# Single rows of the node table fetched by SyncE and ScalarE for 14 gather tiles in place of 5, in a graph attention layer

## The reference

```python
Q, K, V = (x @ Wq + bq), (x @ Wk + bk), (x @ Wv + bv)        # [N, 8 heads, 12]
E = edge_attr @ We + be                                      # [edges, 8, 12]
score = K[src] * Q[dst] / sqrt(12) * E
score = exp(clip(score.sum(-1), -5, 5))                      # [edges, 8]
msg = V[src] * score
h = segment_sum(msg, dst) / (segment_sum(score, dst) + 1e-6)
out = layernorm(x + h)
```

## Time and profile before

| | |
|---|---|
| median of the runs | 999.71 us |
| the profiled execution, its own time | 999.58 us |
| its span, first to last instruction | 997.9 us |
| GpSimd (POOL) busy | 741.4 us, 74% |
| VectorE (DVE) busy | 651.9 us, 65% |
| TensorE (PE) busy | 646.7 us, 65% |
| ScalarE (ACT) busy | 186.5 us, 19% |
| DMA | 165.62 MB, mean 166 GB/s |

### The profile page before, as it was taken

The page is one execution under the profiler, slowest core; times in us unless marked ns, Lnnn a source line. Parts: engine busy times, 40 slices in busy tenths (PEclk is TensorE's granted clock), DMA queues, the critical chain, the costliest instruction groups (busy, mean ns, idle before and its releaser), DMA issues. The chain is left out here.

```text
span 997.9 us, 13968 instructions
## 1 busy us (share of the span) xinstructions
PE 646.7 (65%) x3276; PEld 418.5 (42%) x3276; DVE 651.9 (65%) x1307; ACT 186.5 (19%) x373; POOL 741.4 (74%) x783
## 2 busy tenths in 40 slices
PE   5688778656655665748566666567657664757663
PEld 5564555433433443435333343344434443434443
DVE  6637999666756665766565766566756666657665
ACT  4742222111111111111111111111111111111111
POOL 7777777777777777777777777777777777777772
PEclk9888999888877887886878787877887788887885
DMA  6899776665656556555656556565565565665531
GB/s 196 286 293 244 197 203 176 177 184 156 176 143 170 155 146 177 156 153 159 168 145 167 148 147 171 152 162 156 157 176 142 145 174 149 162 160 140 143 86 42
DMA packets 102425, 165.62 MB, mean 166 GB/s; under 512 B 45725, under 2 KB 65006, under 8 KB 102335
## 3 DMA queue, kind: packets, MB, share of 16 engines
q1 hardware_dynamic: 64399, 84.88, 30.8%
q0 software_dynamic: 36784, 74.86, 28.6%
q10 hardware_dynamic: 1152, 4.92, 1.4%
HBM read 152.18 MB, written 12.39 MB: 165 GB/s over the span
## 5 line engine op out<-in xcount | busy, mean ns | idle before, releaser
L419 POOL DMA_INDIRECT kv<-kv_table,idx x745 | 709.8, 953 | 227.1 <-issue 225.9
L522 PE MATMUL psT<-identity,qe 96*128 96x96 f32 x782 | 111.8, 301 | 292.0 <-DVE qe L861 291.9
L944 DVE TENSOR_TENSOR qke<-psT,kv 128x768 f32<-128x768 f32 (+1 forms) x99 | 93.6, 945 | 288.6 <-DMA kv<-kv_table,idx 287.1
L501 PE MATMUL psE<-ea,we 97*96 97x512 f32 x392 | 268.8, 825 | 0.8 <-ACT kv L641 0.8
L522 PEld LDWEIGHTS psT<-identity,qe 96*128 96x128 f32 x782 | 89.2, 172 | 308.6 <-DVE qe L861 308.4
L571 PEld LDWEIGHTS psA<-place,msg 128*104 128x104 f32 x1536 | 159.9, 179 | 36.0 <-DVE msg L971 26.0
L571 PE MATMUL psA<-place,msg 128*104 128x104 f32 x1536 | 167.0, 264 | 9.9 <-DVE msg L971 9.5
L671 ACT ACTIVATE qe<-psE 96x1024 f32<-96x1024 f32 (+1 forms) x99 | 99.8, 1009 | 231.2 <-PE psE L501 231.2
L685 ACT ACTIVATE msg<-clipped 128x64 f32<-128x64 f32 (+1 forms) x99 | 25.3, 255 | 513.4 <-DVE clipped L959 503.4
L861 DVE TENSOR_TENSOR qe<-psQ,qe 96x1024 f32<-96x1024 f32 (+1 forms) x99 | 118.5, 1197 | 3.7 <-ACT qe L671 3.6
L501 PEld LDWEIGHTS psE<-ea,we 97*96 97x96 f32 x392 | 77.8, 224 | 82.8 <-issue 82.8
(11 more groups left out here) (105 smaller groups left out, 324.9 us busy)
## 6 DMA issues: line engine op xcount, KB each, us to landing
ea<-eaT SPq DMA_DIRECT2D x99, 384.0 KB, 4.1
q_parts<-rel_table SPq DMA_DIRECT2D x99, 252.0 KB
kv<-kv_table,idx POOLq DMA_INDIRECT x745
kv_rows<-kv_table SPq DMA_DIRECT2D x640, 0.8 KB
qwin<-q_table SPq DMA_DIRECT2D x198, 23.6 KB
xb<-xrows SPq DMA_DIRECT2D x24, 144.0 KB
out<-ob SPq DMA_DIRECT2D x24, 144.0 KB
kv_table<-kv ACTq DMA_DIRECT2D x2, 960.0 KB, 8.3
```

Of the source, the lines that this page charges most:

```text
L419: pool.indirect_dma_start(kv[:, k, t], None, kv_table, sources).then_inc(kv_in[k], 16)
L501: last = nc.tensor.matmul(psE[0:D, h, 0:size], we[:], ea[:, k % EAR, edge:edge + size], start=True, stop=True)
L522: last = nc.tensor.transpose(psT[:, t % 2, t // 2 * D:(t // 2 + 1) * D], qe[0:D, k % 2, t * P:(t + 1) * P], identity[0:D, 0:D])
L944: nc.vector.tensor_tensor(qke[:, 0:nt].rearrange("p (t b) d -> p b t d", **by_bank), psT[:, :, 0:nt // 2 * D].rearrange("p b (t d) -> p b ...
```

## The change

14 tiles in place of 5 are left out by GpSimd. Nine of them, those of groups 15, 25, ..., 95, are SyncE's: 13 rows in a turn, 10 turns for a tile (the last has 11 rows), in groups 4 to 93 without a gap. Five, those of groups 22, 38, ..., 86, are ScalarE's: 8 rows in a turn, 16 turns for a tile, in groups 4 to 83, issued by ScalarE after its moves and before the two functions of the root. Both begin in group 4. The buffer `kv_rows` is no tensor of its own any more but lies in `q_full`, which nothing reads after the first stage; ScalarE's first turn waits for that (`q_up`). The list of source numbers that is loaded once, `row_id`, grows from 640 to 1792 numbers. VectorE waits for `rows_up` in 14 groups.

```diff
-BY_ROW = (24, 40, 56, 72, 88)
-ROWS = 8
+SP_ROWS, ACT_ROWS = 13, 8
+SP_TURNS, ACT_TURNS = -(-P // SP_ROWS), -(-P // ACT_ROWS)
+FROM = 4
+SP_TILES = tuple(15 + SP_TURNS * i for i in range(9))
+ACT_TILES = tuple(22 + ACT_TURNS * i for i in range(5))
+BY_ROW = SP_TILES + ACT_TILES
...
-        kv_rows = sb("kv_rows", [P, len(BY_ROW), 2 * D], f32)
+        kv_rows = q_full[:].rearrange("p t d -> p (t d)").rearrange("p (i f) -> p i f", f=2 * D)[:, 0:len(BY_ROW)]
...
+        def load_single_rows(eng, i, j, rows):
+
+            count = min(rows, P - j * rows)
+            edge = i * P + j * rows
+            nodes = nc.values_load_multi_w_load_instructions(
+                row_id[0:1, edge:edge + count], engines=[eng.engine], min_val=0, max_val=N - 1,
+                skip_runtime_bounds_check_because="source nodes of edges are nodes")[1]
+            for p in range(count):
+                eng.dma_start(kv_rows[j * rows + p:j * rows + p + 1, i], kv_table[bass.ds(nodes[p], 1), :]
+                              ).then_inc(rows_in[i], 16)
...
-                        turn = at - (BY_ROW[0] - P // ROWS - 1)
-                        if 0 <= turn < len(BY_ROW) * P // ROWS:
-                            load_single_rows(turn)
+                        turn = at - FROM
+                        if turn == 0:
+                            sp.wait_ge(row_id_in, 16)
+                            sp.wait_ge(kv_out, 16 * len(KV_CHUNKS))
+                        if 0 <= turn < len(SP_TILES) * SP_TURNS:
+                            load_single_rows(sp, turn // SP_TURNS, turn % SP_TURNS, SP_ROWS)
...
+                        turn = at - FROM
+                        if first and turn == 0:
+                            act.wait_ge(row_id_in, 16)
+                            act.wait_ge(q_up, NR // P // QB)
+                        if first and 0 <= turn < len(ACT_TILES) * ACT_TURNS:
+                            load_single_rows(act, len(SP_TILES) + turn // ACT_TURNS, turn % ACT_TURNS, ACT_ROWS)
                         if first and BG <= at < NG and at % BG == 1:
                             block_rstd(U // BG * r + k // BG - 1, BC)
...
-                                dve.wait_ge(rows_up, BY_ROW.index(at) + 1)
+                                dve.wait_ge(rows_up, sum(1 for x in BY_ROW if x <= at))
```

More of the change, by code:

```diff
@@ L333, in _ @@
                     ahead = []
[L335 to L346, removed]
                     def loads(r, k, at):
```

## The result

The changed kernel takes **1137.35 us** (median of 4 runs, 1136.43 to 1139.88) against 999.7 us before (4 runs, 999.14 to 1000.49). The ratio is 1.138, with a 95% interval of 1.136 to 1.140: 138 us slower. The prediction was 1005.8 us, with a range of 995 to 1040. "Slower" was right, the size was not: 131.5 us of the loss were not in the sum. The profiled execution took 1137.81 us, with a span of 1136.1.

The account below looks back on a forecast made before the run. GpSimd's gathers bound the kernel before; with the change SyncE would end last. VectorE's last group 10.2 us later, less a 4.00 us wait, is 6.2 net: 997.9 + 6.2 + 1.7 = 1005.8 us, range 995 to 1040.

Parts of the forecast that it names:

- The step that failed: SyncE's register load each turn: 13 numbers in place of 8 at 36 ns a number, 0.18 us more a group.
- 13 rows as two loads: Bound on SyncE's register load: about one more load a turn, 0.46 us, 41 us over 90 groups.
- The rule that was dismissed: About 200 ns a loaded register on SyncE: five more cost 1.0 us, 74 us more over 90 groups; not adopted.
- SyncE's chain sets the end: SyncE issues rows without rest until 972.4, so VectorE begins group 95 at 974.8; the end comes 6.2 us later net.
- the row pitch: SyncE's time from one row DMA to the next: 0.42 us, so five more rows cost 2.1 us a group.
- The end as forecast: VectorE's last wait, in group 95, is for ScalarE's copy until 974.8; the gathers have long landed by then.
- 15 to 30 forecast: VectorE's waits ahead of `qke` for ScalarE's copy in groups 15, 25, ..., 95: 15 to 30 us.
- The start: SyncE starts group 5's windows at 108.6, and VectorE can't begin group 15 before 197.8, against 170.85 before.
- One stop of GpSimd: GpSimd waits 7.7 us for late queries ahead of group 19, due at 195.3, keeping 3.6 of its 11.3 us gain.
- Rival 2: SyncE's rows cost more, through a second load or the two queues hindering each other: 1016 to 1057 us, chance 0.18.
- Rival 1: SyncE isn't last and GpSimd's end decides: 996.0 us with the stop at group 19, 988.3 without; chance 0.11.
- covered at 8 rows: ScalarE's rows and load, 4.0 to 4.5 us a group, fit its free time and cost nothing at the end.

Follow-up runs that it names:

- e7: Kernel before, SyncE using 8 rows a turn but loading lists of ten kinds (8 to 16 numbers, starts shifted by 0 to 2 numbers): 998.65 us, ratio 1.000.
- e1: Changed kernel with the source list padded so each SyncE turn's 13 numbers start at a multiple of 16 bytes: 1034.6 us, ratio 1.036 against the kernel before.
- e3: Changed kernel without ScalarE's five tiles, SyncE's nine kept: 1135.83 us, ratio 1.137 against the kernel before.
- e5: Changed kernel with 12 rows a SyncE turn, eight SyncE tiles from group 16, ScalarE's five from 24: 992.98 us, ratio 0.994 against the kernel before.
- e6: As e5, but SyncE's tiles are used one group later, from 17, and ScalarE's begin at 22: 990.83 us, ratio 0.993 against the kernel before.
- e4: Changed kernel with SyncE back at its five old tiles of 8 rows, ScalarE's five kept: 993.61 us, ratio 0.994 against the kernel before.
- e8: As e6 for SyncE, but ScalarE takes eight tiles of 12 rows from group 4: 993.98 us, ratio 0.994 against the kernel before.
- e10: As e8, but ScalarE issues its rows behind the root and begins in group 15, with seven tiles: 987.22 us, ratio 0.988 against the kernel before.

## Why the prediction was wrong in size

**The step that failed** is "The register load grows from 8 numbers to 13 ... 36 ns a number: 0.18 more". It measured 2.35 - 0.66 = 1.69 us more (means over 90 and 80 loads), 1.51 above what was priced. 90 x 1.51 = 136 us is the whole miss of 131.5. The cycle agrees: 44.95 - 38.9 = 6.05 us, 1.51 a group.

It failed twice. The slope of 36 ns shared out 712 - 462 = 250 ns among seven numbers; by the count of e7 that is one step and not seven equal shares (e7 had no load of one number). And 250 ns was no firm price. The trace of before had one more line with loads of one number, and they spread as far among themselves:

```profile
L325 SPq TENSOR_LOAD <-block_int x24: 279/540/586, 132.2 to 979.3; - x24
```

With 0.66 + 0.18 = 0.84 priced and 1.17 measured in e1, that mistake is worth (1.17 - 0.84) x 90 = 30 us, and e1 shows it alone: 1034.6 is 28.8 above the prediction. The other part, 103 us, is the start of the list in memory. All loads of numbers from `row_id` in the trace of before began at a multiple of 16 bytes, so no row there could show it; but a tile cut in parts of 13 gives starts that 8 never had, and I bounded the load by "13 rows as two loads", a case about length. The bound below and above was drawn along one axis.

**The rule that was dismissed.** The Trainium skill's Runtime: NRT & Kernel Launch, section Instruction fetch mechanics, has about 200 ns a register even in bulk. It speaks there of register loads that the runtime adds, and not of a kernel's own loads from a list in on-chip memory. For the loads off a 16-byte start the trace agrees: 2.88 / 13 = 0.22 us, and e7 has 0.20. For those on it, it doesn't: 8 numbers in 0.53 to 0.84 (in the kernel before), 0.07 to 0.11 each. By the rule the prediction would have been 1005.8 + 74 = 1080, nearer than mine and still short, because the load of 8 that it starts from was itself a cheap one. The rows told against it at one start and one length; that was no reason to give it no chance among the rivals.

**What held.** SyncE's chain sets the end, from group 5 to the last row of tile 95: the row pitch is 0.416 (0.42), with no rest; the 20.4 us of waits lie ahead of that stretch and behind it. The last row is issued at 1099.48 + 4.75 = 1104.23, and from there to the end of the span it is 1136.1 - 1104.2 = 31.9 us, where the prediction had 1004.1 - 972.4 = 31.7. The end as forecast: VectorE's last wait for the copy, then no wait for gathers. Its nine waits for SyncE's tiles were 12.8 to 20.3 us, a little under the 15 to 30 forecast.

```profile
1105.47 0.36 ACT L701 ACTIVATE kv<-q_full 128x192 f32<-128x192 f32 x1 [11.38 <-DMA q_full<-kv_table]
1105.96 0.96 DVE L955 TENSOR_TENSOR qke<-psT,kv 128x768 f32<-128x768 f32 x1 [20.34 <-ACT kv L701]
```

**The start.** Group 5's windows came at 105.15 (108.6 forecast). Its turn took 115.48 - 105.15 = 10.33 us and not 8.4; the gap of 3.15 us ahead of its rows is the load. VectorE began group 15 at 206.96 and not at 197.8.

**One stop of GpSimd** was wrong. SyncE was slower than GpSimd all along, so its edge features fell behind again and again, and with them the queries:

```profile
171.23 0.95 POOL L424 DMA_INDIRECT kv<-kv_table,idx  x1 [6.59 <-PE psQ L516]
...
195.17 0.94 POOL L424 DMA_INDIRECT kv<-kv_table,idx  x1 [4.26 <-PE psQ L516]
...
215.69 0.95 POOL L424 DMA_INDIRECT kv<-kv_table,idx  x1 [10.81 <-PE psQ L516]
```

The 46 waits hold 140.3 us. They cost nothing on top: the last gather starts at 1095.60, and VectorE's last wait, up to 1105.96, is for the copy. But the first stands at 171, where the prediction had its only one ahead of a gather at 195.3. I had followed what waits for the single rows and not the edge features that SyncE issues behind them.

**Rival 2** (the rows cost more) had the right direction, but neither of its two causes is there. One load stayed one load, and e3 excludes that ScalarE's queue hinders SyncE's. **Rival 1** did not become true with the cheap load alone: in e1 SyncE is still last, at 40.3 us against 39.4. It took one row less as well (e5, e6: 37.5). **ScalarE** was covered at 8 rows, as predicted (e4). At 12 rows in the early groups it isn't (e8 to e10).

**Where the gain went.** Nine gathers fewer were worth 11.3 us, and nine row tiles on SyncE cost 13 rows and a load of 2.35 us in each of 90 groups, on an engine that 8 rows a group had already kept busy for 7.54 of GpSimd's 10.0 us. e10 moves one gather more out of GpSimd's way (735 gathers) than the change does, and takes 987.22 us.

## What to carry to other kernels

Price an instruction by a row with the same length and the same start in memory; a slope between two lengths, or a bound that varies one property only, says nothing of the others, and a new cut of a list (13 in place of 8) changes the start as well. Work given to an engine that feeds every group must leave it shorter per group than the pace-setter, so that one late start dies out and doesn't add up. Begin such work after the stretch in which groups come faster than the steady pace.

## What the runs showed of the hardware

A register load of SyncE from the list in on-chip memory costs by steps of about 0.2 us (e7, the shortest of four): 8 numbers from a 16-byte start in 0.53 us, 12 in 0.76, 16 in 0.99, 11 in 1.16, but 8 from a start 4 or 8 bytes off in 1.68 and 13 in 2.69. ScalarE's loads of 8 numbers from such a start have a median of 0.72. ScalarE's rows of 768 bytes, each 0.4 us behind the last, did not slow SyncE's: SyncE's row DMA had a median of 228 ns with them beside it and without (e3), and 1137.35 us with them stands against 1135.83 without.
